# Inner loops of a four-stage transformer kernel written out one by one

## The reference

```python
# 1: convolution, linear attention with a causal prefix state, gate, 4-expert mixture
x = x + einsum('btd,ed->bte', conv3(x), w_pw)
kv_prefix = cumsum(k_phi[..., :, None] * v[..., None, :], axis=1)
num, denom = q_phi @ kv_prefix, sum(q_phi * cumsum(k_phi, axis=1))
x = x + sigmoid(delta @ w_gate + b_gate) * ((num / (denom + 1e-6)) @ w_o)
# 2: 16 experts with 4-bit weights, two chosen per token
# 3: attention without softmax: (x Wq^T x^T) x
# 4: windowed transformer, 6 layers, 16 heads of 64, window 32
for i in range(6):
    x = attn_layer(shift_tokens(x), Wqkv[i], q_scale[i], k_scale[i], Wo[i]) + x
    x = ffn_layer(shift_tokens(x), ln_g[i], ln_b[i], W1[i], b1[i], W2[i], b2[i]) + x
```

## Time and profile before

| | us |
|---|---|
| median of 3 runs (lowest, highest) | 5664.89 (5663.38, 5672.79) |
| the profiled execution, its own time | 5666.5 |
| its span, first to last instruction | 5664.7 |
| PE busy, DVE busy, ACT busy, POOL busy | 4998.0, 4058.9, 3784.5, 2454.7 |
| mean granted TensorE clock | 0.925 |

### The profile page before, as it was taken

One profiled execution on the slowest core, in us unless ns is written; L12 is line 12 of the kernel. 1 busy time (PEld: TensorE's weight loads), 2 busy tenths in 40 slices (PEclk: granted clock), 3 DMA queues, 4 the chain that ended last, 5 costly groups with the idle time before them and its releaser, 6 DMA issues. The chain is left out here.

```text
span 5664.7 us, 146153 instructions
## 1 busy us (share of the span) xinstructions
PE 4998.0 (88%) x41236; PEld 4163.6 (74%) x41236; DVE 4058.9 (72%) x11142; ACT 3784.5 (67%) x12309; POOL 2454.7 (43%) x3763
## 2 busy tenths in 40 slices
PE   5997895999259998899979999899988999899994
PEld 3665684899248887788868887688877888688873
DVE  4544475777758887788868887688876888688875
ACT  1111342443149997799959998699977999599982
POOL 0000000000246664566636666466655666366661
PEclk7877796999679999999999999999999999899997
DMA  0000110000111111111111111111111111111111
GB/s 20 0 0 15 37 37 1 0 0 0 30 28 25 25 25 47 30 25 25 25 50 25 25 25 49 28 25 25 25 46 28 25 25 25 49 28 25 25 45 31
DMA packets 103075, 144.80 MB, mean 26 GB/s; under 512 B 65245, under 2 KB 72690, under 8 KB 102386
## 3 DMA queue, kind: packets, MB, share of 16 engines
q1 hardware_dynamic: 93410, 107.27, 8.4%
q0 software_dynamic: 9232, 33.12, 1.9%
HBM read 49.13 MB, written 2.10 MB: 9 GB/s over the span
## 5 line engine op out<-in xcount | busy, mean ns | idle before, releaser
L1912 ACT ACTIVATE d_probs<-d_S_ps,d_neg_max 128x96 f32<-128x96 f32 x3072 | 1002.9, 342 | 59.3 <-issue 47.0
L1513 POOL TENSOR_TENSOR d_qk<-d_qk,d_sin_terms 128x512 f32<-128x512 f32 x768 | 961.0, 1273 | 30.5 <-DVE d_sin_terms L2099 30.5
L1688 PEld LDWEIGHTS d_S_ps<-d_kT,d_q_blocks 128*128 128x128 f32 x6144 | 789.5, 192 | 2.2
L1688 PE MATMUL d_S_ps<-d_kT,d_q_blocks 128*128 128x96 f32 x6144 | 788.9, 271 | 0.0
L2099 DVE TENSOR_TENSOR d_qk<-d_A_ps,d_tables 128x512 f32<-128x512 f32 x768 | 527.9, 687 | 236.1 <-ACT d_squares L1868 168.9
L1912 ACT ACTIVATION_READ_ACCUMULATOR d_probs<-d_S_ps,d_neg_max 128x1 f32 x3072 | 638.5, 208 | 0.0
L1645 PE MATMUL d_A_ps<-d_wqkv_hi,d_xT_hi 128*128 128x512 f32 x1152 | 558.8, 485 | 19.5 <-DVE d_sin_terms L2099 14.8
L1868 ACT ACTIVATE d_squares<-d_A_ps 128x512 f32<-128x512 f32 x768 | 462.4, 602 | 127.1 <-PE d_A_ps L1647 126.8
L2099 DVE TENSOR_TENSOR d_sin_terms<-d_A_ps,d_tables 128x512 f32<-128x512 f32 x768 | 523.1, 681 | 0.0
L1920 ACT ACTIVATE d_probsT<-d_PT_ps 96x512 f32<-96x512 f32 (+1 forms) x768 | 460.4, 600 | 80.4 <-PE d_PT_ps L1698 80.4
L1652 PE MATMUL d_T_ps<-d_ident,d_qk 128*128 128x128 f32 x3072 | 482.2, 280 | 33.6 <-POOL d_qk L1550 29.1
(11 more groups left out here) (406 smaller groups left out, 10977.9 us busy)
## 6 DMA issues: line engine op xcount, KB each, us to landing
d_v_early<-d_v SPq DMA_DIRECT2D x192, 256.0 KB, 2.9
d_v_early<-d_v SPq DMA_DIRECT2D x192, 128.0 KB, 2.3
d_tables<-L_ffn_rotary POOLq DMA_DIRECT2D x7, 2048.0 KB, 8.3
d_qk<-L_ffn_Wqkv POOLq DMA_DIRECT2D x21, 512.0 KB, 4.0
d_xs<-d_xb SPq DMA_DIRECT2D x56, 127.0 KB
d_xs<-d_xb SPq DMA_DIRECT2D x96, 63.5 KB
ax_fp_blocks<-L_ffn_blocks_gu SPq DMA_DIRECT2D x16, 256.0 KB, 3.9
ax_fp_scales<-L_ffn_scales_gu SPq DMA_DIRECT2D x64, 64.0 KB, 3.5
```

The lines of the kernel that those rows point to most:

```text
L1513: nc.gpsimd.tensor_tensor(c4[:, :, s, :], c4[:, :, s, :], s4[:, :, 1 - s, :], ALU.add).then_inc(rotated, 1)
L1688: last = nc.tensor.matmul(S[g % 2][:, n * SEEN:(n + 1) * SEEN], qx[:, p, half, :], kT[b][jj][:, p, HALF * half:HALF * half + SEEN], start= ...
L1912: nc.scalar.activation(pr[:, g, n, seen_columns(g)], S[g % 2][:, n * SEEN:(n + 1) * SEEN], ACT.Exp, bias=nmax[:, g, n:n + 1], accum_out=de ...
```

## The change

Python loops take the place of the hardware loops named above, so each tile and each group has its own instructions, with `j` or `g` as a constant. The order of the work on each engine, the waits and the buffers stay. The loop over the 6 layers stays, so `l` is still in a register. `tiles_of_layer` now writes out all 32 tiles.

```diff
@@ linear attention: POOL; PE, ACT and DVE likewise with J - 1 @@
-                    with pool.Fori(0, J) as j:
+                    for j in range(J):
                         for b in range(B):
@@ tiles_of_layer @@
-            with engine.Fori(0, J // 2 - 1) as i:
-                for jj in range(2):
-                    for b in range(B):
-                        tile(i * 2 + jj, jj, b, pair=i)
-            tile(J - 2, 0, 0)
-            tile(J - 2, 0, 1)
+            for j in range(J - 1):
+                for b in range(B):
+                    tile(j, j % 2, b, pair=j // 2)
             tile(J - 1, 1, 0, lead=1)
             tile(J - 1, 1, 1, lead=0)
@@ SP @@
-                    with sp.Fori(0, J // 2 - 1) as i:
-                        for jj in range(2):
-                            shift_tile(i * 2 + jj, jj)
-                    shift_tile(J - 2, 0)
+                    for j in range(J - 1):
+                        shift_tile(j, j % 2)
                     shift_tile(J - 1, 1, last=True)
...
-                    with sp.Fori(0, GROUPS - 1) as g:
+                    for g in range(GROUPS):
                         shift_group(g)
-                    shift_group(last_group)
@@ feed-forward groups, PE; ACT likewise @@
-                    with pe.Fori(0, GROUPS // 2 - 1) as i:
-                        for gp in range(2):
-                            g = i * 2 + gp
-                            hidden_units(g + 1, 1 - gp)
-                            outputs(g, gp)
+                    for g in range(GROUPS - 2):
+                        hidden_units(g + 1, (g + 1) % 2)
+                        outputs(g, g % 2)
@@ feed-forward groups, DVE @@
-                    with v.Fori(1, GROUPS // 2 - 1) as i2:
-                        for gp in range(2):
-                            group(i2 * 2 + gp, gp)
+                    for g in range(2, GROUPS - 2):
+                        group(g, g % 2)
```

More of the change, by code:

```diff
@@ L750, in tile @@
                         nc.tensor.matmul(o_b[:, 0:D], aT[:], wo[:], start=True, stop=True).then_inc(o_ps, 1)
-                    with pe.Fori(0, J - 1) as j:
+                    for j in range(J - 1):
                         for b in range(B):
@@ L785, in tile @@
                         nc.scalar.activation(aT[:], T_b[:, 0:P], ACT.Copy).then_inc(aT_ready, 1)
-                    with act.Fori(0, J - 1) as j:
+                    for j in range(J - 1):
                         for b in range(B):
@@ L861, in tile @@
                         nc.vector.scalar_tensor_tensor(row, gt[:], 0.5, row, ALU.mult, ALU.add).then_inc(x2_ready, 1)
-                    with v.Fori(0, J - 1) as j:
+                    for j in range(J - 1):
                         for b in range(B):
@@ L1459, in shift_tile @@
                         shift_rows(j, 1)
-                    with sp.Fori(0, J // 2 - 1) as i:
-                        for jj in range(2):
-                            shift_tile(i * 2 + jj, jj)
-                    shift_tile(J - 2, 0)
+                    for j in range(J - 1):
+                        shift_tile(j, j % 2)
                     shift_tile(J - 1, 1, last=True)
-                    last_group = GROUPS - 1
                     def shift_group(g):
@@ L1474, in shift_group @@
                         shift(g * 2, 2, shift_main)
-                        if g is not last_group:
+                        if g < GROUPS - 1:
                             sp.wait_ge(f_xn, (l * GROUPS + g) * 4 + 8)
@@ L2069, in group @@
                             split_group(m0 + (g + 1))
-                    with act.Fori(0, GROUPS // 2 - 1) as i2:
-                        for gp in range(2):
-                            group(i2 * 2 + gp, gp)
+                    for g in range(GROUPS - 2):
+                        group(g, g % 2)
                     group(GROUPS - 2, 0, more=1)
```

## The result

The changed kernel takes 5594.73 us in the median (5584.04 to 5603.8, 4 runs), the one before 5667.73 (4 runs, the three shown above and one more): a ratio of 0.987, with a 95% interval of 0.985 to 0.989. The profiled execution took 5594.9 us, with a span of 5593.3. The forecast was 5599 for the median and 5600.5 for the profiled execution.

The account below looks back on a forecast made before the run. PE was taken to bound the kernel, stalled at attention's back edges by ACT's instruction loads. 5666.5 - 46 - 17 - 2 - 1 = 5600.5, less 1.6 gave a median of 5599 us; own range 5592 to 5608, whole range 5582 to 5626.

Parts of the forecast that it names:

- step 1: Attention tiles: the 36 back edges go, 1.3 us each, from ACT's wait for instructions; 46 us less (43 to 47).
- DVE has 3 us of slack a tile: Attention: said beside DVE's 16.9 us of idleness at 36 back edges, in taking only ACT's jump as dear.
- step 2: Attention tiles: wait counts need a constant, not the loop's register; 0.10 us a tile, 28 tiles, 6 layers, 17 us less.
- Tile 28: First attention tile behind the loop, already in the new form, 17.27 us; cited for edges alone (chance 0.25, 5616 us).
- the single tile 29: Attention tile already in the new form, 17.17 us against 17.26 to 17.27 in the loop; basis for 0.10 a tile.
- step 3: Attention: PE loads some 24 tiles more in each layer, with the load running ahead of the sequencer; costed at nothing.
- The slower rival: Attention: PE has to wait at 190 more loaded pieces; 250 us more and 66 less, 5850 us; chance 0.04.
- step 4: Linear attention: PE's jump of 215 ns goes at 14 places; 2 us less, 3.7 at most; clock rhythm left at 0.
- steps 5 and 6: Feed-forward back edges and address arithmetic, 1 us less; SP's loops for row shifts and early values, nothing.

## Why the prediction was right, step by step

- **The edges (step 1, 46 us).** Right in the sum: edge less steady was 18.545 - 17.273 = 1.27 us, 36 of them 45.8, and after the change the old edges differ from the rest by 0.02. Wrong in the share: the step gave it all to ACT. ACT's load of instructions makes 0.96 us of it, DVE's jump 0.31, shown by the two kernels that write out ACT, and ACT and DVE. "DVE has 3 us of slack a tile" was the weak sentence. It did no harm, since the change removes both. Wrong too was the wait by which ACT's lateness reaches PE: the step had PE wait for a bank ahead of the next scores. PE's waits there for the exponentials are unchanged (51.6 us before, 50.8 after, 186 each). It waited 1.27 us at the turning of `x`, for ACT's copy of the values, and this is the wait that went, from 56.6 us to 11.4.
- **Cheaper register arithmetic (step 2, 17 us).** Right, and 0.127 us a tile instead of 0.10, which is 21 us for 168 tiles. The place was the one named: one wait more there put 0.125 back. Of the 0.127, 0.106 comes from PE's code alone, and that is the 0.105 by which the bare place got shorter. The other 0.02 is not ascribed: a steady tile of 17.26 instead of 17.27 comes also where ACT's or DVE's code was only moved. Tile 28 was no counter-example, but the reason given for it was wrong: with DVE's code moved and PE's the same it takes 17.14, and with PE alone written out still 17.26. Resting the step on the single tile 29 was in part luck: in the kernel with only the linear attention written out that same tile takes 17.33.
- **Loading code in sequence (step 3, nothing).** Right: q8 brought 224 packets more, where 190 were reckoned, and PE's steady tiles run at 17.15 beside it. The slower rival is gone with that. Two periods of each layer, the same in all six, are 0.14 and 0.11 us longer than the rest, 1.5 us in all; whether a load makes them was not tested.
- **Linear attention (step 4, 2 us).** 3.5 us less were seen, but kernels with an unchanged linear attention spread over 13 us in that stage, and the kernel after with one covered wait more on PE, whose linear attention is the changed one, took the 434.7 of before. So the step is neither borne out nor refuted.
- **Feed-forward and shifts (steps 5 and 6, 1 us).** Between the last attention result and the last feed-forward input the six layers took 364.2 us after and 359.7 before: no gain to be seen, and the other kernels that keep the loop over layers lie between 359 and 366. The turn of a layer costs what it cost, as was said; PE's jump there (line 1716) still takes 3.5 us in the middle.

The profiled execution was expected at 5600.5 and took 5594.9; some 4 of the 5.6 us are step 2's. What the prediction missed altogether is that a cheaper way to the first step existed: the stall depended on where ACT's body lies, and 120 idle instructions ahead of it take 36 x (18.545 - 17.566) = 35 us out of the edges of their profiled execution. That execution is 30.8 us shorter than the one of the kernel before: the attention tiles are 36.5 shorter, the linear attention is 2.4 and the way from layer to layer 2.2 longer. By the timed runs the kernel gained some 26 us, 0.45% (0.31 to 0.59) of 5666.

## What to carry to other kernels

A steady period read from one instruction per tile, inside a pass and across the back edge, gives a loop's cost directly; then look at each engine's sequencer for the time from the branch to its next instruction. A jump of some 3 us there is a load of instructions, and it comes and goes with the position of the body, so any edit ahead of a loop can make or mend it: compare traces and not totals. Where the bounding engine's queue has run empty, each instruction of its sequencer costs 0.1 us of the whole here, and 16 fewer elsewhere in the tile gained nothing. A single tile's length is weak evidence: here it moved by up to 0.16 us with its own code unchanged.

## What was not expected of the hardware

- The same loop with the same body jumps in 2.9, 2.4 to 2.7 or 0.2 us by its position alone, and a change in another stage's code moved it to a cheap place by accident, for 36 us at the edges.
- Three jumps of other engines (PE's of 0.2 us, POOL's and SP's) cost nothing, and DVE's, with 0.5 us of idleness, cost 0.31 us.
- With constants in place of registers a wait can become dearer: the steady tile was 17.190 with the layers written out and 17.146 with the layers' loop, since a register instruction can carry a wait that otherwise takes an instruction of its own.
- PE loads three times the instructions (329 packets and not 105), and its steady tile is at 17.146 beside it.
